# Keys and values projected in a stage of their own, and the softmax sums taken by TensorE in three cross-attention layers

## The reference

```python
q = norm(x) @ Wq.T + bq          # 2 x 512 x 512
k = ctx @ Wk.T + bk              # 2 x 1024 x 512, ctx is an input
v = ctx @ Wv.T + bv
p = softmax(q_h @ k_h.T / sqrt(32))   # per head; layer 1: masked, scores clipped to +-50
x = x + tanh(g) * ((p @ v) @ Wo.T + bo)
```

## Time and profile before

| what | value |
|---|---|
| median of 3 runs (lowest to highest) | 3253.7 us (3251.09 to 3257.65) |
| the profiled execution: time, span | 3245.69 us, 3244.0 us |
| mean granted TensorE clock in it | 0.92 of full |
| TensorE matmul busy | 2705.8 us, 83% of the span |
| VectorE, ScalarE, GpSimd busy | 1725.0, 1173.0, 918.0 us |
| attention of layer 1 (542 to 944 us): TensorE busy | 338.23 of 402 us |
| attention of layer 2 (1560 to 2070 us) | 435.16 of 510 us |
| attention of layer 3 (2275 to 2764 us) | 419.08 of 489 us |

### The profile page before, as it was taken

One profiled execution on the slowest core, in us unless ns is written; L12 is line 12 of the kernel. 1 busy time (PEld: TensorE's weight loads), 2 busy tenths in 40 slices (PEclk: granted clock), 3 DMA queues, 4 the chain that ended last, 5 costly groups with the idle time before them and its releaser, 6 DMA issues. The chain is left out here.

```text
span 3244.0 us, 35880 instructions
## 1 busy us (share of the span) xinstructions
PE 2705.8 (83%) x11495; PEld 1656.5 (51%) x11495; DVE 1725.0 (53%) x3039; ACT 1173.0 (36%) x2506; POOL 918.0 (28%) x436
## 2 busy tenths in 40 slices
PE   7998698999745499999689987588689988599895
PEld 3555586644223366555454543366454543477563
DVE  2453675577665899893655653411555653344212
ACT  0111222566614788781134444111144443221110
POOL 0000000588231010100057663122256663221112
PEclk9989899999977699999799998789799999699998
DMA  6220212422100100100332220432432120212613
GB/s 221 80 95 23 72 67 90 99 70 59 53 30 0 52 27 27 52 26 14 102 70 52 48 59 17 166 113 90 143 70 57 43 59 17 78 39 94 214 65 110
DMA packets 101257, 232.26 MB, mean 72 GB/s; under 512 B 22512, under 2 KB 27120, under 8 KB 99696
## 3 DMA queue, kind: packets, MB, share of 16 engines
q1 hardware_dynamic: 88624, 189.46, 19.5%
q0 software_dynamic: 12480, 40.90, 3.8%
HBM read 142.74 MB, written 30.67 MB: 53 GB/s over the span
## 5 line engine op out<-in xcount | busy, mean ns | idle before, releaser
L1489 POOL TENSOR_TENSOR L_attn_total<-L_attn_total,L_attn_probs 128x2048 f32<-128x2048 f32 x120 | 546.3, 4552 | 152.3 <-ACT L_attn_probs L1444 148.0
L1523 DVE TENSOR_REDUCE L_attn_row_max<-L_attn_rows_ps 128x1 f32<-128x512 f32 x512 | 335.8, 684 | 267.8 <-PE L_attn_rows_ps L1329 264.9
L1444 ACT ACTIVATE L_attn_probs<-L_attn_s_ps 128x512 f32<-128x512 f32 x512 | 292.3, 596 | 418.7 <-PE L_attn_s_ps L1349 414.7
L1349 PE MATMUL L_attn_s_ps<-L_attn_q_stack,L_attn_k_stack 98*128 98x512 f32 (+1 forms) x768 | 378.6, 529 | 39.5 <-DMA L_attn_q_stack<-L_attn_ml 33.5
L436 PE MATMUL L_ffn_hidden<-L_ffn_x_high,L_ffn_up_high 128*128 128x512 f32 x688 | 295.6, 430 | 100.0 <-DVE L_ffn_routes L352 54.2
L318 ACT ACTIVATE L_ffn_sums<-sims 128x128 f32<-128x128 f32 x1024 | 315.5, 390 | 50.3 <-DVE L_ffn_routes L331 26.1
L1489 POOL TENSOR_TENSOR L_attn_total<-L_attn_probs 128x2048 f32<-128x2048 f32 x20 | 91.0, 4552 | 789.2 <-ACT L_attn_probs L1444 789.2
L1349 PEld LDWEIGHTS L_attn_s_ps<-L_attn_q_stack,L_attn_k_stack 98*128 98x128 f32 (+1 forms) x768 | 141.8, 194 | 264.3 <-issue 128.6
L436 PE MATMUL L_ffn_hidden<-L_ffn_x_low,L_ffn_up_high 128*128 128x512 f32 x688 | 272.8, 397 | 0.0
L1362 PE MATMUL L_attn_o_ps<-L_attn_probs,L_attn_values 128*32 128x512 f32 x1536 | 210.8, 621 | 26.4 <-ACT L_attn_probs L1444 22.8
L1329 PE MATMUL L_attn_rows_ps<-L_attn_k_stack,L_attn_q_stack 96*128 96x512 f32 x512 | 207.6, 440 | 29.3 <-DVE L_attn_row_max L1523 27.3
(11 more groups left out here) (272 smaller groups left out, 4227.3 us busy)
## 6 DMA issues: line engine op xcount, KB each, us to landing
L_attn_k_stack<-L_attn_kh SPq DMA_DIRECT2D x192, 128.0 KB, 2.4
L_attn_ctxT<-in_ctxT SPq DMA_DIRECT2D x8, 2048.0 KB, 12.8
L_attn_abs_in<-in_L_ffn_w SPq DMA_DIRECT2D x12, 1024.0 KB, 9.7
L_attn_k_stack<-L_attn_kl SPq DMA_DIRECT2D x96, 128.0 KB, 2.4
L_attn_q_stack<-L_attn_qh SPq DMA_DIRECT2D x192, 64.0 KB, 2.0
L_ffn_xg<-x_slots POOLq DMA_DIRECT2D x46, 256.0 KB, 3.2
y_slots<-L_ffn_y_sb POOLq DMA_DIRECT2D x46, 256.0 KB, 2.3
L_ffn_up_all<-in_L_ffn_w SPq DMA_DIRECT2D x16, 704.0 KB, 13.6
```

The lines of the kernel that those rows point to most:

```text
L1349: nc.tensor.matmul(s_ps[:, v % S_SLOTS, :], k_stack[0:depth, n % 2, h, kt * P:(kt + 1) * P], q_stack[0:depth, n % 2, h, :], start=True, st ...
L1444: nc.scalar.activation(probs[:, g % P_SLOTS, h, :], s_ps[:, v % S_SLOTS, :], ACT.Exp, **kinds).then_inc(exp_done, 1)
L1489: nc.gpsimd.tensor_tensor(total[:], first, probs[:, g % P_SLOTS], ALU.add).then_inc(added, 1)
L1523: nc.vector.tensor_reduce(row_max[:, r // HALVES_K, r % HALVES_K:r % HALVES_K + 1], rows_ps[:, r % R_SLOTS, :], AX_X, ALU.max, negate=True ...
```

## The change

A new block, `keys_values_block`, runs once, between the attention and the feed-forward part of layer 0, while `ctxT` is still in SBUF. It projects the keys and values of layers 1 to 3 from high and low parts (three fp32r matmuls for each product: high x high, high x low, low x high) and stores the keys, already split, and the values in HBM (`kd`, `vd`). The attention blocks of layers 1 to 3 no longer load the context. SyncE loads the keys of a set from `kd` with three DMAs of 32 partitions each (all four heads at once) and the values with one. For set n + 2 this comes behind the stack of the queries, which is now 12 DMAs. Only the 4 query chunks stay among the units, at units 12, 14, 16 and 18, in one bank.

The sums are now taken by TensorE in every set, in front of each `pv`, in a bank of their own (`sums_ps`). ScalarE copies that bank to SBUF behind its copy of the output bank, and VectorE inverts the copy. GpSimd only normalises. There are four slots of `probs` and not three. Output weights are loaded early, to a tensor of their own.

```diff
+def keys_values_block(env, layers, kd, vd):
+    L, UNITS, W = len(layers), 16, 8
...
+        terms = ((w_hi, c_hi), (w_hi, c_lo), (w_lo, c_hi))
...
+            @block.tensor
+            def _(pe):
+                for l in range(L):
+                    for u in range(UNITS):
...
+                        pe.wait_ge(w_ready, W * l + DC + f + 1)
...
+                        if i >= 2:
+                            pe.wait_ge(kl_done, i - 1)
+                        steps = [(c, w, x) for c in range(DC) for w, x in terms]
+                        for q, (c, w, x) in enumerate(steps):
+                            last = nc.tensor.matmul(k_ps[:, i % 2, :], w[:, f, c * P:(c + 1) * P],
+                                                    x[:, c, j * HALF:(j + 1) * HALF], start=(q == 0), stop=(q == len(steps) - 1))
+                        last.then_inc(k_psum, 1)
+                        if i >= 2:
+                            pe.wait_ge(v_done, i - 1)
+                        for q, (c, w, x) in enumerate(steps):
+                            last = nc.tensor.matmul(v_ps[:, i % 2, :], x[:, c, u * P:(u + 1) * P], w[:, place(l, c), :],
+                                                    start=(q == 0), stop=(q == len(steps) - 1))
+                        last.then_inc(v_psum, 1)
...
+    def load_keys(self, sp, n):
+        for r, part in enumerate((0, 1, 0)):
+            sp.dma_start(self.k_stack[32 * r:32 * (r + 1), n % 2].bitcast(F32),
+                         self.kd[n, part].rearrange("(h p) k -> p h k", p=32)).then_inc(self.k_loaded[n % 2], 16)
...
-    SUMMED = range(SETS - 1 if less_max_rows else SETS - 2, SETS)
+    CHUNK_AT = {u: (QUERIES, c) for c, u in enumerate((12, 14, 16, 18))}
...
                     if n >= 2:
                         sp.wait_ge(scores_done, UNITS * (n - 1))
                     for h in range(HG):
-                        for dst, parts in ((k_stack, (kh, kl, kh)), (q_stack, (qh, qh, ql))):
-                            for r in range(3):
-                                sp.dma_start(dst[HD * r:HD * (r + 1), s, h, :].bitcast(F32),
-                                             parts[r][HD * h:HD * (h + 1), :].bitcast(F32)).then_inc(stacked[h], 16)
+                        for r, part in enumerate((qh, qh, ql)):
+                            sp.dma_start(q_stack[HD * r:HD * (r + 1), s, h, :].bitcast(F32),
+                                         part[HD * h:HD * (h + 1), :].bitcast(F32)).then_inc(stacked[h], 16)
+                    if n >= 2:
+                        inputs.load_keys(sp, n)
...
                     if q == 0 and i == 0:
                         pe.wait_ge(stacked[h], STACKS * (n + 1))
+                        pe.wait_ge(inputs.k_loaded[n % 2], KEYS * (n // 2 + 1))
...
+                    if kt == 0 and n:
+                        pe.wait_ge(total_taken, n)
+                    for h in range(HG):
+                        last = nc.tensor.matmul(sums_ps[HD * h:HD * (h + 1), :], ones[:], probs[:, g % P_SLOTS, h, :],
+                                                start=(kt == 0), stop=(kt == KT - 1))
+                    last.then_inc(summed, 1)
...
                     nc.scalar.copy(heads[:], o_ps[:]).then_inc(taken, 1)
+                    act.wait_ge(summed, KT * (n + 1))
+                    if n:
+                        act.wait_ge(inverted, n)
+                    nc.scalar.copy(total[:], sums_ps[:]).then_inc(total_taken, 1)
...
-                for n, i in FIRST_ITEMS[:EARLY]:
+                for n, i in FIRST_ITEMS:
                     low(n, i)
-                for j in range(EARLY * DC):
-                    if less_max_rows:
-                        for r in range(j * ROWS // (EARLY * DC), (j + 1) * ROWS // (EARLY * DC)):
-                            maximum(0, r)
-                    if j % DC == DC - 1:
-                        low(*FIRST_ITEMS[EARLY + j // DC])
+                if less_max_rows:
+                    for r in range(ROWS):
+                        maximum(0, r)
```

372 lines of the change are left out of this document (216 added, 156 removed).

## The result

The changed kernel takes 3629.6 us (median of 4 runs, 3625.9 to 3631.0) where the kernel before takes 3255.7 us beside it: a ratio of 1.115, 95% interval 1.113 to 1.117. The profiled execution took 3629.05 us, its span is 3627.3 us.

The account below looks back on a forecast made before the run. TensorE was taken as nearly full in layer 1, with closed chains elsewhere; 3245.7 + 286 - 19 - 18 + 1 + 2 x 58 = 3612, plus 8 for the median: 3620 us, range 3560 to 3690.

Parts of the forecast that it names:

- The new block: After layer 0's attention: 1152 matmuls at 0.226 us, TensorE setting the pace, plus start and tail: +286 us (270 to 302).
- Layer 1, start: Layer 1 attention: with fewer chunks ahead, the first exponential starts near 575 instead of 594.46: -19 us.
- Layer 1, sets: Layer 1 attention: a set takes 35.1 us for 38.17, six times, judged from the old last set: -18 us.
- Layers 2 and 3, sets without the wait: Layers 2 and 3: set 6's 40.9 us plus sums and chunks gives 48.8 us a set before any new wait.
- sets without the wait are much under 47 us, which would mean that sums hide: Layers 2 and 3: a listed sign that the prediction is wrong, with TensorE's sums hidden rather than lengthening sets.
- All eight sums: Layers 2 and 3: TensorE's sums ahead of pv lengthen VectorE's idle time in every key tile, 6.9 us a set.
- The four chunks: Layers 2 and 3: the remaining query chunks, 3.5 us on TensorE, lengthen each set by 2.0 us.
- The wait: Layers 2 and 3: TensorE's row products wait for late keys, 10.4 us (7.6 to 14) in each of 12 sets.
- The clock behind the wait: Layers 2 and 3: some 4 us at half clock after each wait, costing 0 to 2 us; nothing was added.
- The rival with half clock through the set: Layers 2 and 3: each wait leaves TensorE at half clock through most of the set, perhaps 8 us more: 3716 us, chance 0.08.
- Together: Layers 2 and 3: with the wait, sets 1 to 5 become 59.2 us for 49.0, +51 us per layer.
- Layers 2 and 3, start: Layers 2 and 3: the turned maxima come near 1620.7 instead of 1628.91: -8 us in each layer.

Follow-up runs that it names:

- the best version that was run: Changed kernel with three key slots; in layers 2 and 3 GpSimd sums sets 0 to 5 with three slots of probabilities, elsewhere TensorE sums: 3411.4 us, ratio 1.048.

## Why the prediction was right, and where it was lucky

The forecast of 3620 us missed by 10, and the sum for the profiled execution, 3612, by 17. By its own steps:

- **The new block**: +284.4 for +286, and 285 by itself. Right in size and in reason: 0.227 us a matmul, 17 us ahead of the first for the 15 and a barrier of 2. No run shows the barriers and the tail (8 us together) one by one, only the sum.
- **Layer 1, start**: -20.9 for -19. Right, and by the mechanism that was named: ScalarE stands before its first exponential at a split that waits for the copies of set 0.
- **Layer 1, sets**: 34.6 for 35.1. The last set before the change was a good measure of what all sets become. But the reading "TensorE is nearly full, and its 20 chunks are what fills it" left out what has no slack in that set: GpSimd's chain, 33.1 us of work and some 5 of waits, is as long as the set of 38.17, and with 4 chunks and GpSimd's additions a set still takes 39.4. The forecast was right because the set it measured, the last, had its sums on TensorE.
- **Layers 2 and 3, sets without the wait**: 44.5 for 48.8, the largest error. It is one of the prediction's own signs of being wrong: "sets without the wait are much under 47 us, which would mean that sums hide". All eight sums were taken to lie open, 6.9 us, against 1.0 for the one that goes, because key tiles run at the pace of VectorE plus its idle time. That holds in the middle of the set, where a key tile with row products and no chunk takes 5.7 us as forecast, but not in all eight tiles: in place of 5.9 us the change of sums costs 3.7 (44.5 with TensorE's, 40.85 with GpSimd's). The four chunks were priced at 2.0 and show nothing: 40.85 us with them, for 40.91 in set 6 of the kernel before, which has none.
- **The wait**: 12.7 us on average, 13.1 in the set shown, for 10.4. The transfer was sized well: issue to release 9.8 us for 9.1, and 213 to 231 GB/s at a full share, in windows of this stretch and the next ones, for the 226 of the earlier trace rows. What failed is when TensorE arrives: 4.2 us behind the first copy (2063.67 - 13.11 - 2046.37), not 6.1. The prediction took 1932.09 for the arrival in the earlier trace rows and added 0.9 for the sums; but that row starts after 1.15 us of waiting, so TensorE had arrived at 1930.94, 4.0 behind the first copy, and the sums hardly showed.
- **The clock behind the wait**: up to 2.4 us a set, which was put at nothing. Some 1 us of it is the clock, by the runs with matmuls without use. The rival with half clock through the set came up in part, in the longest set (64.7 us, mean granted clock 0.82). Its wait ends at 2183.95, and the clock was back at 0.93 before it fell again:

```profile
2194.00:2198.00 4.00, 4.00 (x18) 0.91 (x19) 2.56 (x4) 0.00 (x0) 0.00 (x0) 0.59 0.00 0
```

- **Together**: 40.9 + 3.7 + 12.7 + 2.4 = 59.7 us for the usual set, for 59.2. The base, the chunks and the sums were 4.2 us too high, the wait and the clock 4.7 too low. So the set is right to 0.5 us by errors that cancel, and that is luck; either pair alone would have moved the time by 50 or 56 us, which the range of 3560 to 3690 still held. Some sets are longer than the usual one, and the mean of ten, 60.7, is 1.5 above the forecast. That is most of the 7.6 and 5.7 us by which layers 2 and 3 exceed their +58.
- **Layers 2 and 3, start**: 4.6 us sooner for 8 (the turned maxima at 1877.42, 74.9 us behind the start of the stage, for 79.4 before). From there to the first copy, set 0 in the main, layer 2 gains another 3.9 us, which was put at nothing.
- **Not foreseen**: 3.9 us in layer 0's feed-forward, cause open.

The Trainium skill's figure for 32 partitions, 189 GB/s (SBUF — State Buffer, section "Door 1: The DMA port swizzle"), was weighed in the prediction. The runs decide for the trace: 213 to 231 GB/s in windows of the late stretch, with three queued loads of 32 partitions each, and 376 in the window of the block, with stores from 128 partitions and loads to them. The trace agrees with the page on the ratio, somewhat over half, and not on the figure.

## What to carry to other kernels

Take the price of a wait from both ends: when the data land, and when the waiting engine arrives. The arrival is the end of its work before the waiting row, not the start of that row, which has an old wait in it. A second buffer is no prefetch if it is refilled only when the first stage that reads it is over; a third slot gave back 181 us where a better order of issue gave 82. Before a set's length is put down to its busiest engine, follow the chains around the others: beside a TensorE busy 36 of 38 us, GpSimd with 33 of 38 stood in a closed chain as long as the set. Before work is moved into a stage of its own, multiply it out: 285 us in one place must be given back by the places it leaves, and there the chunks had been lying in waits, so that 343 us of TensorE time and the move of the sums together gave back some 127 in the best version that was run.
